# Token rows that carry their gate, added to the output by the scatter itself

## What is computed

```python
h = _layernorm(x) * (1 + cb) + sb
x = x + gb * _L1_ffn_ref(h, ...)
# _L1_ffn_ref: t = rmsnorm(h) * norm_w;  logits = t @ gate_w.T + gate_b
# vals, idx = top_k(logits, 4);  G = softmax(vals) at idx, 16 experts
# y[e] = act(t @ w1[e].T + b1[e]) @ w2[e].T + b2[e]
# returns h + sum over e of G[:, e] * y[e]
```

## Time and profile before

| | before |
|---|---|
| median of 3 runs | 1166.97 us (1166.55 to 1167.17) |
| the profiled execution | 1166.73 us |
| its span, first to last instruction | 1164.9 us |
| PE, PEld busy | 1056.2, 892.9 us |
| DVE, ACT, POOL busy | 704.2, 663.9, 421.1 us |
| DMA | 81.33 MB, mean 70 GB/s |

### The profile page before, as it was taken

How to read it: one execution, slowest core, us unless ns; L and a number is a source line. 1 busy time by engine, 2 the same in 40 slices (tenths; PEclk the granted TensorE clock), 3 DMA queues, 4 the chain that set the end, 5 groups by cost and what they waited for, 6 DMA issues and landing times.

```text
span 1164.9 us, 21347 instructions
## 1 busy us (share of the span) xinstructions
PE 1056.2 (91%) x6755; PEld 892.9 (77%) x6755; DVE 704.2 (60%) x2350; ACT 663.9 (57%) x1864; POOL 421.1 (36%) x379
## 2 busy tenths in 40 slices
PE   7999999999999999999999999987633999999950
PEld 4668888878887887887887888874423999999940
DVE  2453555666575576566657547646342788888845
ACT  2646675567576656756756665754212777766720
POOL 3312412333235235232523413500312455555546
PEclk9999999999999999999999999996566999999985
DMA  9931000000001001000100100108205465556556
GB/s 318 281 112 55 2 1 20 1 25 34 19 2 57 19 1 58 1 19 1 57 1 1 58 1 1 58 21 359 93 10 163 72 97 98 96 94 99 90 83 215
DMA packets 51934, 81.33 MB, mean 70 GB/s; under 512 B 7278, under 2 KB 44718, under 8 KB 50542
## 3 DMA queue, kind: packets, MB, share of 16 engines
q1 hardware_dynamic: 34939, 56.77, 14.5%
q0 software_dynamic: 15280, 21.70, 11.1%
q10 hardware_dynamic: 1602, 1.48, 0.5%
HBM read 56.10 MB, written 28.47 MB: 73 GB/s over the span
## 4 chain that ended last, share of the span: by engine, by line
PE 83%; issue 5%; DVE 5%; POOL 3%; DMA 2%; ACT 1%; SPq 1%; POOLq 0%; DVEq 0%; ACTq 0%
PE bank L1017 12%; PE bank L981 9%; PE bank L954 9%; PE bank L1029 5%; PE bank L944 5%; PE bank L971 5%; PE bank L962 4%; PE bank L931 3%; PE bank L899 3%; PE bank L804 2%; PE bank L942 2%; PE bank L924 2%; PE bank L972 2%; PE bank L813 2%; PE bank L883 2%
## 5 line engine op out<-in xcount | busy, mean ns | idle before, releaser
L1834 POOL DMA_INDIRECT accD<-SC,BC x79 | 124.3, 1574 | 125.2 <-DVE SC L1699 109.4
L1017 PE MATMUL bank<-SC 128*128 128x128 f32 x1264 | 155.8, 277 | 1.0 <-ACT SC L1286 1.0
L1794 POOL TENSOR_TENSOR RB<-RA 128x512 f32<-128x512 f32 x64 | 66.9, 1046 | 247.2 <-DVE RA L1585 247.1
L1017 PEld LDWEIGHTS bank<-SC 128*128 128x128 f32 x1264 | 149.1, 194 | 1.2 <-ACT SC L1286 1.2
L981 PE MATMUL bank<-RA,RB 128*128 128x256 f32 x512 | 135.8, 388 | 0.3
L1279 ACT ACTIVATE SC<-RA,nw 128x512 f32 x158 | 105.5, 715 | 32.4 <-issue 32.3
L954 PE MATMUL bank<-RA 128*128 128x256 f32 x512 | 122.1, 381 | 0.0
L954 PEld LDWEIGHTS bank<-RA 128*128 128x128 f32 x512 | 94.1, 190 | 15.1 <-issue 1.8
L981 PEld LDWEIGHTS bank<-RA,RB 128*128 128x128 f32 x512 | 89.8, 190 | 16.4 <-issue 3.8
L1769 POOL TENSOR_TENSOR qs<-qs,half 128x4 f32<-128x4 f32 x64 | 66.2, 1034 | 96.4 <-DVE qs L1591 90.3
L1164 ACT ACTIVATE RB<-bank,sm,qs 128x128 f32<-128x128 f32 x128 | 58.3, 456 | 53.2 <-DVE sm L1601 52.2
(11 more groups left out here) (239 smaller groups left out, 2428.9 us busy)
## 6 DMA issues: line engine op xcount, KB each, us to landing
BC<-xsD SPq DMA_DIRECT2D x79, 136.5 KB, 2.6
BC<-modD SPq DMA_DIRECT2D x16, 512.0 KB, 3.7
RA<-in_w SPq DMA_DIRECT2D x4, 2048.0 KB, 19.6
accD<-SC SPq DMA_DIRECT2D x2, 2176.0 KB, 12.6
RA<-accD SPq DMA_DIRECT2D x16, 256.0 KB, 3.9
RB<-in_w2b SPq DMA_DIRECT2D x1, 2560.0 KB, 12.9
RA<-in_L_attn_Wq SPq DMA_DIRECT2D x1, 2048.0 KB, 13.7
RA<-in_L_attn_Wo SPq DMA_DIRECT2D x1, 2048.0 KB, 19.6
```

Of the source, the lines that this page charges most:

```text
L1017: m = pe.matmul(ps[:, 128 * j:128 * j + 128], WS[:, n % 2, c, 128 * j:128 * j + 128], XT[:, n % 2, c * 128:c * 128 + 128], start=(c == 0), ...
L1794: pool.tensor_tensor(sq, q, q, ALU.mult).then_inc(mine("q_sq", p), 1)
L1834: pool.indirect_dma_start(accD[n % 2][:, :], bass.IndirectOffsetOnAxis(XB[:, n % XB_RING, 256:257].bitcast(U32), 0), YB[:, n % 3, :], None ...
```

## The change

- A row in xsD has 529 floats, 2116 B: behind the 273 come the 256 of the block's gb row, times 0.5. A new ScalarE stage f_gb writes them into `xsc` (now 1058 floats) after f_src; the sends wait for it, and so does the load of the next rows into that slot of BC.
- y_out multiplies result, gate and gb in one scalar_tensor_tensor.
- SyncE stores X(b) into out right after f_x(b), in the plan's order, instead of at the end.
- y_add adds even blocks into out itself (every add waits for store(7)) and odd ones into one accumulator. Pad rows have token numbers over 2047 and are dropped by a bounds check.
- The end is `merge`: four DMAs from GpSimd that add accD to out, from DRAM to DRAM, 64 rows of 8 KB each. gb_in, y_in, y_sum, y_x and the second accumulator go.
- The ring of block loads has 9 places (xb also waits for f_gain(6)).

```diff
-NBLK, REG, ROW = 79, 2048 + 128, 273
-XB_RING, XB_AHEAD = 12, 6
+NBLK, REG, ROW = 79, 2048 + 128, 529
+XB_RING, XB_AHEAD = 9, 6
...
-        "SP": "bc .1 mod_store .1 acc_zero 2.8 zrow_store 8.0",
+        "SP": "store .1 bc .1 mod_store .1 acc_zero 2.8 zrow_store 8.0",
...
         yield do("f_src", b, after=[("f_send", 1, b - 1, 1, 3), ("f_t", 1, b - 1), ("g_t", b - 1)] * prev)
+        yield do("f_gb", b, aside=True)
...
-                yield do("f_send", 1, b, i, k, slot=b % 4, by=16, aside=True)
+                yield do("f_send", 1, b, i, k, slot=b % 4, by=16, aside=True, after=[("f_gb", b)])
...
-            yield do("bc", 1, b + 2, slot=4 + b % 2, by=16, aside=True)
+            yield do("bc", 1, b + 2, slot=4 + b % 2, by=16, aside=True, after=[("f_gb", b)])
         yield do("f_x", b)
+        yield do("store", b, by=16)
...
-    p.add("gb_in", by=16 * NB)
...
+    p.add("merge", by=16 * 4)
...
-        accD = [nc.dram_tensor(f"accD{i}", (2048 + 128, 256), F32, kind="Internal").ap() for i in range(2)]
+        accD = nc.dram_tensor("accD", (2048, 256), F32, kind="Internal").ap()
...
             def xb(n):
...
+                on.wait_ge(*done("f_gain", NB - 2))
...
-                sp.dma_start(XB[:, n % XB_RING, 0:273], xsD[bass.ds(r, 128), :]).then_inc(mine("xb", n), 16)
+                sp.dma_start(XB[:, n % XB_RING, 0:ROW], xsD[bass.ds(r, 128), :]).then_inc(mine("xb", n), 16)
...
             def store(b):
-                on.wait_ge(*done("y_x", b))
+                on.wait_ge(*done("f_x", b))
                 sp.dma_start(out_v[:, b, :, :], X[:, 2 * b:2 * b + 2, :]).then_inc(mine("store", b), 16)
...
+            def f_gb(b):
+                on.wait_ge(*done("bc", 1, b))
+                if b:
+                    on.wait_ge(*done("f_send", 1, b - 1, 1, 3))
+                act.activation(route(1)["src"][:, :, 273:529], row(1, b, 768), ACT.Copy, scale=0.5).then_inc(mine("f_gb", b), 1)
...
-                dve.tensor_scalar(YB[:, n % 3, :], psum("y_out", n)[:, 0:256], XB[:, n % XB_RING, bass.ds(ex[n] + 257, 1)], 0.5, ALU.mult, ALU.mult).then_inc(mine("y_out", n), 1)
+                dve.scalar_tensor_tensor(YB[:, n % 3, :], psum("y_out", n)[:, 0:256], XB[:, n % XB_RING, bass.ds(ex[n] + 257, 1)], XB[:, n % XB_RING, 273:529], ALU.mult, ALU.mult).then_inc(mine("y_out", n), 1)
...
+                on.wait_ge(*done("store", NB - 1))
...
-                pool.indirect_dma_start(accD[n % 2][:, :], bass.IndirectOffsetOnAxis(XB[:, n % XB_RING, 256:257].bitcast(U32), 0), YB[:, n % 3, :], None, compute_op=ALU.add).then_inc(mine("y_add", n), 16)
+                pool.indirect_dma_start((out_r, accD)[n % 2], bass.IndirectOffsetOnAxis(XB[:, n % XB_RING, 256:257].bitcast(U32), 0), YB[:, n % 3, :], None,
+                                        bounds_check=2047, oob_is_err=False, compute_op=ALU.add).then_inc(mine("y_add", n), 16)
...
+            def merge():
+                on.wait_ge(*done("y_add", NBLK - 2))
+                on.wait_ge(*done("y_add", NBLK - 1))
+                for i in range(4):
+                    pool.dma_start(out_r[512 * i:512 * i + 512, :].rearrange("(a c) n -> a (c n)", c=8), accD[512 * i:512 * i + 512, :].rearrange("(a c) n -> a (c n)", c=8),
+                                   accum_op=ALU.add, max_dma_last_dim=8192).then_inc(mine("merge"), 16)
```

More of the change, by code:

```diff
@@ L26 @@
         "mod_on_pe": "mod_mm modc_mm", "mod_on_dve": "silu mod_out mod_clamp mod_one modc_out",
-        "route_on_pe": "f_t f_gate f_rank s_mm s_t", "route_on_act": "f_sq f_src f_ht f_hb f_sig f_exp s_tanh s_at",
+        "route_on_pe": "f_t f_gate f_rank s_mm s_t", "route_on_act": "f_sq f_src f_ht f_hb f_gb f_sig f_exp s_tanh s_at",
         "route_on_dve": "f_var f_top f_hot f_gw f_sum f_macc f_w f_pos s_act s_x",
@@ L46 @@
               "p_t .33 scores .78 q_mm 1.73 q_ss .9 pv .65 wo .87 qk_mm 1.73 vv_mm .87 ls_mm .65 num .56 o1_t .22 wo1 .87",
-        "ACT": "g_out .4 h_mod 1.05 k_sq 1.6 v_out .6 f_ht .62 f_hb .62 f_sig .2 f_sq .9 f_src .9 f_exp .7 s_tanh .3 s_at .38 d_tanh .32 d_at .95 "
+        "ACT": "g_out .4 h_mod 1.05 k_sq 1.6 v_out .6 f_ht .62 f_hb .62 f_sig .2 f_sq .9 f_src .9 f_gb .6 f_exp .7 s_tanh .3 s_at .38 d_tanh .32 d_at .95 "
                "silu_t .3 gate_t .2 s_exp 1.15 p_tout .5 p_norm .82 o_out .4 el_exp .64 vv_out .4 o1_out .4",
@@ L472, in build @@
         macc_set = ctx.enter_context(nc.semaphore("macc_set"))
[L473 removed]
+        own = {e: ctx.enter_context(nc.semaphore(f"{e}_own")) for e in ("dve", "act")}
         def done(stage, *key):
@@ L662, in build @@
         out_v = out.rearrange("b (t p) d -> p b t d", p=128)
+        out_r = out.rearrange("b s d -> (b s) d")
         block = ctx.enter_context(nc.Block())
@@ L708, in bc @@
                     on.wait_ge(*done("f_gain", b - 2))
+                    on.wait_ge(*done("f_gb", b - 2))
                     on.wait_ge(*done("f_add", 1, b - 2))
@@ L715, in acc_zero @@
                 on.wait_ge(*done("zeros"))
-                for i in range(2):
-                    sp.dma_start(accD[i].rearrange("(a p) n -> p a n", p=128), zz.unsqueeze(1).broadcast_to([128, 17, 256])).then_inc(mine("acc_zero"), 16)
+                sp.dma_start(accD.rearrange("(a p) n -> p a n", p=128), zz.unsqueeze(1).broadcast_to([128, 16, 256])).then_inc(mine("acc_zero"), 16)
             def zrow_store():
@@ L752, in w2_end @@
                 sp.dma_start(W2[:, 10:16, :, :].rearrange("p e c n -> p (e c n)"), I["w2b"][:, 5120:8192]).then_inc(mine("w2_end"), 16)
[L754 to L764, removed]
-                    sp.dma_start(YG[:, b % 4, i, :, :], accD[i][256 * b:256 * b + 256, :].rearrange("(t p) n -> p t n", p=128)).then_inc(mine("y_in", b), 16)
             def store(b):
-                on.wait_ge(*done("y_x", b))
+                on.wait_ge(*done("f_x", b))
                 sp.dma_start(out_v[:, b, :, :], X[:, 2 * b:2 * b + 2, :]).then_inc(mine("store", b), 16)
             run = {"mod_store": mod_store, "bc": bc, "acc_zero": acc_zero, "zrow_store": zrow_store,
-                   "pad_sp": pad_sp, "xb": xb, "w12": w12, "w2_end": w2_end, "gb_in": gb_in, "y_in": y_in, "store": store}
+                   "pad_sp": pad_sp, "xb": xb, "w12": w12, "w2_end": w2_end, "store": store}
             for stage, *key in plan.order:
@@ L776, in _ @@
             on.wait_ge(*done("store", NB - 1))
+            on.wait_ge(*done("merge"))
         @block.tensor
```

49 lines of the change are left out of this document (11 added, 38 removed).

## The result

| | before | after |
|---|---|---|
| median | 1167.07 us (1166.55 to 1170.21, 4 runs) | 1177.55 us (1175.46 to 1178.31, 4 runs) |
| ratio | | 1.008 [1.0057, 1.0104] |
| span of the profiled execution | 1164.9 us | 1176.0 us |

What follows compares the result with a forecast made beforehand. It took TensorE to bound the full stretches and expert loop, and a chain of waits the stretches at 850 to 893 and after 1119. Terms: 11.6 + 0.5 - 2.5 - 13.1 - 1.5 = -5.0, so 1162.0 us; range 1152 to 1172.

Steps and rivals of the forecast that it cites:

- Pads, +11.6: Front of the experts: SyncE's pads start later and carry more bytes, last landing at 899.8 against 888.2, +11.6 us.
- +9.5 (issue only): Lower bound of the pads' cost: SyncE's last pad goes out 9.5 us later by issue alone.
- First loads, +0.5: Before the first expert block: larger block loads take longer, seen once, +0.5 us (0.3 to 0.9).
- The shorter ring of 9 delays no load: Expert loop: a block load waits only for an add nine blocks back, so no delay was priced.
- have two blocks, 5.7 us: Expert loop: adds landing in 3.7 to 6.0 us have 5.7 us before the next on their accumulator.
- rival 3: Expert loop: doubled loads push adds over two periods, 6.2 us per pair instead of 5.7, +18, 1180 us; chance 0.05.
- gb loads gone, -2.5: End of the loop: without eight broadcast loads beside them the last adds land sooner, -2.5 us (-4 to -1).
- Tail, -13.1: After the last add's landing: four accumulating DMAs replace reads, adds and stores, 17.4 instead of 30.5 us, -13.1 (-17.4 to -3.6).
- The reordered plan, -1.5: Planner's changed order on every engine from block 3 on: -1.5 us (-3 to +3).
- TensorE is full there, so order alone moves nothing until the last wo: Stretch before the last wo: the new order was priced at no time on a full TensorE.
- Done in the 2.37 us gap: After the last wo: block 6's h_t, qk, vv and four transposes fit TensorE's gap while VectorE makes block 7's residual.
- Block 7's chain starts some 3 us earlier: After the last wo: the new order starts block 7's chain some 3 us earlier, block 6's later.

Runs made afterwards that it cites:

- the experiment with the store of block 7: Changed kernel with the store of block 7 moved behind SyncE's eight pads: ratio 1.0031 to the kernel before.
- the short loads: Changed kernel whose block loads bring only 273 of each row's 529 floats, leaving out the factor gb: ratio 0.9997 to the kernel before.
- the bf16 rows: Changed kernel with gb in bf16 (1604-byte rows), twelve block-load places, store of block 7 behind SyncE's pads: 1160.48 us, 0.993; on the fourth chip 0.9949.
- the second profile of the kernel before: The kernel before, run once more unchanged: 1168.83 us.
- the kernel before in the new order: Kernel before with only the changed kernel's order of work on every engine: ratio 1.0033 on the first chip, 1.0083 on the fourth.
- the changed kernel in the order of before: Changed kernel with f_gb and stores taking no place in the planner's clocks, so engines keep the kernel before's order: ratio 1.0072.
- the bf16 one in the order of before: Kernel with gb in bf16 and store of block 7 behind pads, in the kernel before's order: 0.9862 on the third chip, 0.988 on the fourth.

## Why the prediction was wrong, step by step

- **Pads, +11.6: the size was right, +10.1** (10.0 to 11.4 more than before in six other profiles with the same rows and order on SyncE). The path was not: the forecast let the bytes bind, and its bound "+9.5 (issue only)" is what happened. The last pad's issue moved by 10.1 us and its landing took 3.48 us as before. The bytes come next, at 24.0 against 27.9 us, as the experiment with the store of block 7 shows.
- **First loads, +0.5: right** (3.5 against 3.0).
- **"The shorter ring of 9 delays no load" and "have two blocks, 5.7 us": this step failed, by 7.3 us** (6 to 13 over the profiles). The load was priced by its own landing, and the adds' time was taken from the earlier trace rows, the last adds, which have no block load beside them. The 6.03 us of the add beside the gb loads was a sign of what loads do to adds, and was counted only as a gain of the change. With 265 KB loads beside them the adds of the slower target land in 4.9 to 5.3 us (medians of five profiles) instead of about 4. To that come some 0.85 us until the next add on the same target is issued (in the loop's chain 5.40 from issue to landing and 6.25 from issue to issue, 984.76 to 991.01 on GpSimd). From issue to issue a pair takes 5.9 to 6.2 us in the mean between 1000 and 1110 us, against 5.74 before. That the width of the loads is the cause is shown by the short loads (loop 228.4) and by the bf16 rows (228.5). This is the mechanism of rival 3. It had priced 6.2 us per pair as well, but named it a landing and gave it a chance of 0.05. It gave 18 us where 6 to 13 came, as not every pair takes 6.2.
- **y_out, 0, and f_gb, 0: right.** y_out stayed at 0.48 us. The last f_gb took 0.61 us in front of a ScalarE that then waited 0.69 more for TensorE.
- **gb loads gone, -2.5: -4.2**, just outside the stated -4 to -1. From the end of the loop to the last landing: 14.9 before (14.2 in the second profile of the kernel before, which would make -3.5), 10.7 after.
- **Tail, -13.1: right, -12.4** (30.5 to 18.1, where 17.4 was forecast). Some of this is luck. The merge's data took 10.8 us against the 12 taken, and the end behind it 5.4 us (1170.6 to 1176.0) against the 3.3. The 3.3 were also misread: the last store's data in rows 10 ends in the 30th slice, at 1161.25, which leaves 3.65. The whole merge took 12.5.
- **The reordered plan, -1.5: this step failed, with the wrong sign.** "TensorE is full there, so order alone moves nothing until the last wo" overlooked that a full engine in a new order can meet an operand that is not ready (1.6 us at g_t). "Done in the 2.37 us gap" overlooked that the moved work has its own chain through VectorE and ScalarE and could not use the gap. And "Block 7's chain starts some 3 us earlier" was not so: from its residual in the first layer to its residual in the second it takes 73.8 us in the order of before and 77.8 in the new one, the means over 5 and 11 profiles (71.0 to 76.4 and 75.9 to 79.6). By the ratios the order costs 3.9 to 9.8 us.

With the measured terms the sum is 10.1 + 0.5 + 7.3 - 4.2 - 12.4 = +1.3, plus 3.9 to 9.8 for the order: +5.2 to +11.1. Measured by ratio it is +9.3 and +9.4 on two chips. So the sum closes only within the spread of the order's price. The bf16 version with the first chip's order price adds up too: 3.9 + 3.2 (pads) + 0 (loop) - 16 = -8.9; measured -8.2 on that chip.

**Still open:** why the order costs 4 us on one chip and 8 to 10 on another. In the kernel before in the new order the pads alone took 20.3 us on the fourth chip and 17.2 on the first, but the kernel before has no profile on the fourth, so how much of this the order makes is not shown. Open too is why the changed kernel in the order of before (1.0072) gained almost nothing by it. Its interval, 1.0043 to 1.01, leaves room for up to 4 us; its eight runs range over 10.5 us, and its profile reaches the last wo at 785.4, later than the three of the new order on that chip (779.9 to 783.0), with a granted clock of 0.95 from 50 to 100 us. What slows an add beside a larger load inside the DMA engines was not separated either, nor why the adds of only one target are slow. A packet of the adds' queue takes the engines no longer (30.9% of 50 us for 2320 packets here, 107 ns each; 37.6% for 2586 with short loads, 116 ns), so it seems to wait for its turn rather than to work longer; that is a reading, no experiment.

**The best version** is the bf16 one in the order of before: 0.988 [0.986, 0.99], 14 us faster than the kernel before on the same chip. It rounds gb to bf16, which the kernel before does not.

## What to carry to other kernels

A transfer that is hidden itself can still set the pace, by what it does to the transfers beside it. Price the neighbour's latency from a row where both run, and compare it with the period that the neighbour has, reissue included. The loss need not be in proportion: half of the extra bytes cost the loop nothing. When two paths end close together, removing the later one gives back only their difference (3.9 of 10.1 us at the pads). And when a change alters a planner's order, run the old kernel in the new order as a change of its own; it cost 4 to 10 us here.

## Not expected of the hardware

- An accumulating transfer from DRAM to DRAM moved 2.10 MB in 10.8 us, 194 GB/s of results, with 8 KB rows; 107 ns per 1 KB row with small ones, less than the 131 ns of a scatter-add's packet. The profile counts 2.10 MB read and 2.09 MB written for it (65.40 and 38.95 MB against 63.30 and 36.86 without it), so whether the second operand's read loads the memory isn't shown.
- A VectorE add of 128x256 in f32 took 1.96 us in place of 0.42 beside a GpSimd multiply of 128x512. It ends at 848.98, just behind the multiply's end at 848.69 (847.58 + 1.11), as if it had been held until then. The Trainium skill ("SBUF — State Buffer", section "SBUF: two separate sides") has an exclusive lock between the two engines for such pairs, which the one that starts first holds. The trace agrees with a lock, but its times do not show that order: VectorE is recorded as starting 0.56 us earlier and still lost. The profile's times on GpSimd are rough, so f_gain may have held the port before its recorded start. No experiment here took the two apart.
- The kernel before took 1167 to 1168 us in the first runs and on the first two chips named above, and 1177 on the third and fourth. In the profiles of those two the last wo ended at 788.6 to 794.0 us in place of 779.9 to 785.4. Part of that is waits such as the one at 575.99: from 500 to 600 us TensorE was busy for 95.0 us in the changed kernel's second profile and for 98.2 in its first. Part is clock: the granted clock there was 0.98 and 1.00. Why a chip should bring more waits is not shown.
